# An attention and feed-forward kernel: the first stack loaded pair by pair, scores ahead of the first gate, and one gate and up pair moved into the first row

## What is computed

```python
xn = _layernorm(x, axis=-1)
x = x + _L0_attn_ref(xn, qkv_w, qkv_b, proj_w, proj_b) + _L0_ffn_ref(xn, w_gate, w_up, w_down)
# attention, 16 heads of 16 channels
qkv = xn @ qkv_w + qkv_b
attn = softmax(einsum('bnhd,bmhd->bhnm', q, k) * scale)
out = einsum('bhnm,bmhd->bnhd', attn, v) @ proj_w + proj_b
# feed-forward, hidden size 768, integer weights times 1/127
h = silu(xn @ wg.T) * (xn @ wu.T);  ffn = h @ wd.T
```

## Time and profile before

| | |
|---|---|
| median of 3 runs | 574.96 us |
| profiled execution | 576.71 us |
| its span | 574.9 us |
| PE, DVE, ACT, POOL busy | 97%, 81%, 73%, 53% of the span |
| mean granted clock of PE | 0.994 |

### The profile page before, as it was taken

The page is one execution under the profiler, slowest core; times in us unless marked ns, Lnnn a source line. Parts: engine busy times, 40 slices in busy tenths (PEclk is TensorE's granted clock), DMA queues, the critical chain, the costliest instruction groups (busy, mean ns, idle before and its releaser), DMA issues.

```text
span 574.9 us, 13815 instructions
## 1 busy us (share of the span) xinstructions
PE 555.6 (97%) x4844; PEld 334.2 (58%) x4844; DVE 464.9 (81%) x601; ACT 418.0 (73%) x573; POOL 305.1 (53%) x286
## 2 busy tenths in 40 slices
PE   7898899999999999999999999999999999998896
PEld 6656456565655557556665656555665556554453
DVE  5797777888878888888878889888978888788732
ACT  3666865888668975888668875788758886787572
POOL 3283536755564745755566554846467555355120
PEclk9899989999999999999999999999999999999999
DMA  8896086363854368371872449371873438520101
GB/s 235 254 244 146 3 216 179 57 141 118 236 110 105 62 198 206 56 164 71 245 143 69 98 156 241 62 156 29 228 189 61 93 138 227 99 57 21 57 2 38
DMA packets 55119, 74.89 MB, mean 130 GB/s; under 512 B 5680, under 2 KB 28208, under 8 KB 55088
## 3 DMA queue, kind: packets, MB, share of 16 engines
q1 hardware_dynamic: 55088, 74.47, 52.0%
HBM read 40.90 MB, written 33.03 MB: 129 GB/s over the span
## 4 chain that ended last, share of the span: by engine, by line
PE 90%; DVE 4%; ACT 3%; issue 1%; DMA 1%; SPq 0%; ACTq 0%
PE dense L1280 23%; PE o_bank L1254 22%; PE st_bank L1221 16%; PE dense L1324 14%; PE s_bank L1238 11%; PE dense L1264 2%; DVE neg_max L1004 1%; ACT probs L841 1%; PE dense L1393 1%; DMA probs<-in_L_attn_qkv_w 1%; PE dense L1380 0%; DVE w_dl L1033 0%; PE s_bank L1221 0%; ACT w_qkvh L830 0%; ACT probs L927 0%
## 5 line engine op out<-in xcount | busy, mean ns | idle before, releaser
L1004 DVE TENSOR_REDUCE neg_max<-s_bank 128x2 f32<-128x1024 f32 x250 | 304.9, 1220 | 73.9 <-PE s_bank L1238 72.8
L841 ACT ACTIVATE probs<-st_bank 128x1024 f32<-128x1024 f32 x250 | 256.4, 1026 | 112.6 <-PE st_bank L1221 109.4
L1254 PE MATMUL o_bank<-probs,v_ones 128*32 128x512 f32 x1024 | 137.1, 607 | 0.1
L1221 PEld LDWEIGHTS st_bank<-q_stack,k_stack 50*128 50x128 f32 x500 | 47.7, 184 | 131.7 <-ACT probs L841 82.1
L1221 PE MATMUL st_bank<-q_stack,k_stack 50*128 50x512 f32 x500 | 118.0, 466 | 5.3 <-ACT probs L841 5.0
L1238 PE MATMUL s_bank<-k_stack,q_stack 48*128 48x512 f32 x500 | 108.9, 429 | 0.9 <-DVE neg_max L1004 0.7
L742 POOL TENSOR_TENSOR hid_tl<-gated,hid_th 128x512 fp32r<-128x512 f32 x48 | 61.7, 1285 | 35.2 <-ACT hid_th L941 35.2
L736 POOL TENSOR_TENSOR gated<-gated,hid 128x512 f32<-128x512 f32 x48 | 61.7, 1285 | 28.7 <-DVE gated L1026 19.8
L1280 PE MATMUL dense<-xn_tl,w_gh 64*128 64x512 f32 x176 | 61.9, 391 | 0.0
L1280 PE MATMUL dense<-xn_tl,w_uh 64*128 64x512 f32 x176 | 61.9, 391 | 0.0
L1238 PEld LDWEIGHTS s_bank<-k_stack,q_stack 48*128 48x128 f32 x500 | 47.4, 185 | 20.7 <-DVE neg_max L1004 8.4
(11 more groups left out here) (152 smaller groups left out, 886.2 us busy)
## 6 DMA issues: line engine op xcount, KB each, us to landing
q_stack<-q_spread SPq DMA_DIRECT2D x64, 192.0 KB, 4.7
k_stack<-k_spread SPq DMA_DIRECT2D x64, 192.0 KB, 5.2
q_spread<-qk_parts SPq DMA_DIRECT2D x16, 512.0 KB, 3.8
k_spread<-qk_parts SPq DMA_DIRECT2D x16, 512.0 KB, 3.5
q_spread<-qk_parts SPq DMA_DIRECT2D x16, 256.0 KB, 4.1
k_spread<-qk_parts SPq DMA_DIRECT2D x16, 256.0 KB, 2.0
resid<-in_L_attn_x SPq DMA_DIRECT2D x16, 256.0 KB, 4.3
out<-resid SPq DMA_DIRECT2D x15, 256.0 KB, 2.2
```

Of the source, the lines that this page charges most:

```text
L841: nc.scalar.activation(probs[:, s % 2, 2 * half:2 * half + 2, :], transposed_bank(row, s, half)[:, :, :], ACT.Exp, scale=SCALE).then_inc(e ...
L1004: nc.vector.tensor_reduce(neg_max[:, g % 2, :, NT * pair + qt], score_bank(row, half)[:, :, :], AX_X, ALU.max, negate=True).then_inc(max_d ...
L1221: done = nc.tensor.matmul(transposed_bank(row, s, half)[:, r, :], k_stack[rows, pair, P * kt:P * (kt + 1)], q_stack[rows, pair, :], start= ...
L1254: done = nc.tensor.matmul(o_bank[32 * j:32 * (j + 1), :], v_ones[:, kt, 8 * (g // 2) + 2 * j + g % 2, :], probs[:, (s - 1) % 2, j, :], sta ...
```

## The change

Four edits. The first stack (group 0 of row 0) is loaded in two pairs with a semaphore each, eight transfers instead of four, and the scores wait for their pair only. The load of x for row 1 goes behind q's and k's spread writes instead of ahead of them. The first gate and up products go behind the first scores instead of ahead of them. The fourth gate and up leave the preparation for step 0 of row 0, which gets a table of its own: its ups stand in steps 0, 2 and 3, its q and k of index 0 in steps 5 and 6 (4 and 5 before), and its token split one step later.

```diff
+ROW0 = [
+    (0, 0, "up", KH + 3, 0, (2,)), (0, 0, "gate", KH + 3, 0, (0,)),
+    (1, 0, "v", 1, 0, (1, 2)),
+    (2, 0, "up", 4, 0, (1,)), (2, 0, "gate", 4, 0, (0,)), (2, 0, "max", 1, 0, (2,)),
+    (3, 0, "up", 5, 0, (2,)), (3, 0, "gate", 5, 0, (1,)),
+    (5, 0, "q", 0, 1, (1, 0)),
+    (6, 0, "k", 0, 1, (2, 1)), (6, 0, "max", 2, 0, (0,)),
+] + STEADY[STEADY.index((7, 0, "q", 1, 1, (2, 0))):]
...
-TOGETHER = {("up", i): ("gate", i) for i in range(KH)}
+TOGETHER = {("up", i): ("gate", i) for i in range(2 * KH)}
...
     (4, 0, "q", 1, 1), (5, 0, "k", 1, 1),
-    (7, 0, "gate", 0, 1), (8, 0, "up", 0, 1),
-    (10, 2, "gate", 1, 1),
-    (11, 2, "up", 1, 1),
+    (10, 1, "gate", 0, 1), (10, 2, "up", 0, 1),
+    (11, 1, "gate", 1, 1), (11, 2, "up", 1, 1),
     (12, 1, "wdown", 0, 1), (12, 1, "wdown", 1, 1), (12, 2, "gate", 2, 1),
     (13, 1, "wdown", 2, 1), (13, 2, "up", 2, 1),
-    (14, 1, "max", 0, 1), (14, 2, "gate", 3, 1),
-    (15, 1, "v", 0, 1), (15, 2, "up", 3, 1),
+    (14, 1, "max", 0, 1),
+    (15, 1, "v", 0, 1),
...
 TOKENS_SPLIT_AT = ((2, 1), (3, 1))
+ROW0_TOKENS_SPLIT_AT = ((3, 1), (4, 1))
...
     if like < 0:
         return FIRST
-
+    if like == 0:
+        return ROW0
...
+            def load_first_stack():
+
+                sp.wait_ge(ones_ready, 1)
+                for pair in range(2):
+                    for stack, parts in ((q_stack, q_spread), (k_stack, k_spread)):
+                        both = parts[0:P].rearrange("(p r e d) a n -> r e (d a) p n", p=2, r=2, e=2)[:, 0]
+                        for half in range(2):
+                            first = HALF * half
+                            sp.dma_start(stack[first:first + STACK, pair].bitcast(F32),
+                                         both[half][:, pair]).then_inc(first_stack_in[pair], 16)
...
                 if row.has(1):
                     spread_heads(row, "k", 0)
+                if row.like == -1:
+
+                    sp.wait_ge(dense_done, count(row, any_chunk, kind="xn", index=1))
+                    load_x(1)
...
-                if p == 0 and qt == 0:
-                    pe.wait_ge(stack_in[g], 16 * STACK_LOADS * (row.at + ahead + 1))
+                if g == 0 and row.like == -1:
+                    if qt == 0:
+                        pe.wait_ge(first_stack_in[p], 16 * STACK_LOADS)
+                elif p == 0 and qt == 0:
+                    pe.wait_ge(stack_in[g], 16 * STACK_LOADS * (row.at + ahead + (g > 0)))
```

More of the change, by code:

```diff
@@ L344, in build @@
         stack_in = [sem(f"stack_in{g}") for g in range(NG)]
+        first_stack_in = [sem(f"first_stack_in{pair}") for pair in range(2)]
         max_in = [sem(f"max_in{g}") for g in range(NG)]
@@ L456, in splits_at @@
                 return []
-            items = [("xn", n) for n in range(KC) if (step, slot) == TOKENS_SPLIT_AT[n] and row.has(0) and row.has(1)]
+            places = ROW0_TOKENS_SPLIT_AT if row.like == 0 else TOKENS_SPLIT_AT
+            items = [("xn", n) for n in range(KC) if (step, slot) == places[n] and row.has(0) and row.has(1)]
             if slot == 1:
@@ L591, in load_stack @@
             def load_stack(row, g):
-                if row.like == -1:
-                    sp.wait_ge(ones_ready, 1)
-                else:
+                if row.like >= 0:
                     sp.wait_ge(st_done, 2 * STEPS * row.at + 2 * NT * (g + 1))
@@ L643, in step @@
                     sp.dma_start(w_last, proj_w[P:2 * P]).then_inc(w_last_in, 16)
[L644 to L648, removed]
+                if row.has(0) and row.has(2):
                     if row.like == 0:
@@ L667, in step @@
                     heads_spread(row, 0)
+                if row.like == -1:
+                    load_first_stack()
+                elif row.has(1):
                     load_stack(row, 0)
@@ L741, in hidden_low @@
                 pool.wait_ge(hid_high, number(row, "up", m))
-                nc.gpsimd.tensor_tensor(hid_t[1][:, m, :], gated[:, m % 2, :], hid_t[0][:, m, :].bitcast(F32),
+                nc.gpsimd.tensor_tensor(hid_t[1][:, m % KH, :], gated[:, m % 2, :], hid_t[0][:, m % KH, :].bitcast(F32),
                                         ALU.subtract).then_inc(hid_low, 1)
@@ L940, in hidden_high @@
                 act.wait_ge(hid_product, number(row, "up", m))
-                nc.scalar.activation(hid_t[0][:, m, :], gated[:, m % 2, :], ACT.Copy).then_inc(hid_high, 1)
+                nc.scalar.activation(hid_t[0][:, m % KH, :], gated[:, m % 2, :], ACT.Copy).then_inc(hid_high, 1)
             def step(row):
@@ L1409, in spec_of @@
                 if kind == "up":
-                    return (banks, lambda h, a, k: (w_u, w_g)[h][a][:, k, tile(i)], lambda h, b, k: xn_t[b][:, k, :],
+                    return (banks, lambda h, a, k: (w_u, w_g)[h][a][:, k, tile(i % KH)], lambda h, b, k: xn_t[b][:, k, :],
                             terms_of(STATIONARY_EXACT if exact else SPLIT, KC))
```

## The result

The changed kernel took a median of **579.38 us** (578.99 to 580.23, 4 runs) beside 574.91 us for the kernel before (574.55 to 575.86, 4 runs): ratio 1.0077, 95% interval 1.0060 to 1.0095. That is slower, by 4.5 us where 1.4 had been forecast, and just above the upper end of the range. The profiled execution took 580.23 us, with a span of 578.3 us at a granted clock of 0.994. Run again on another chip, unchanged, the same kernel had a ratio of 1.0102 (1.0081 to 1.0123).

What follows compares the result with a forecast made beforehand. PE, busy 97% of the span, was taken as the bound, with VectorE at the preparation's end. The terms -2.4+0.6+3.2+0 = +1.4 gave profiled 578.1, median 576.4 us (forecast case, chance 0.35); range 573.2 to 579.2.

Steps and rivals of the forecast that it cites:

- First stack and x load: Preparation: first pair by about 23, first maximum about 26.5; 3 us slack, so the extra SP issues cost nothing.
- I estimate 0.7 us of VectorE gaps: End of the preparation: time given back because the first hidden tile stands behind 2.1 us of ScalarE work.
- End of the preparation: Decision 1.2 us earlier, at 44.0, then 1.2 us to the first product: row 0 starts at 45.2 instead of 47.58, -2.4 us.
- third rival: The rival "slower by more", chance 0.25; its second condition was thin work around the decision lowering the clock again, +1.45 us.
- Fourth pair in row 0: Row 0, steps 3 to 6: with the moved gate and up pair 15.5 us instead of 14.89, +0.6 us.
- k one step later: PE waits before transposed scores (8,0) for group 2's maxima, 2.2 to 3.7 us, taken as +3.2; late bound a 2.0 us landing.
- the later stack costs nothing behind the stall: Row 0: the next row's stack is later too, but PE asks for it in step 10, after the stall: nothing.
- Clock: Row 0: slow step 7 goes, but the lower level follows the wait in step 8: 0, between -1.45 and +1.45 us.
- slower by more: Timed runs before had no slow step 7, or thin work lowers the clock: 577.8 us, both 579.3; chance 0.25.

Runs made afterwards that it cites:

- trace with filled gaps: Changed kernel with idle PE transpositions, 8 before the first maxima's transposition and 20 before transposed scores (8,0), waits kept: 577.25 us, ratio 1.0054.
- second trace of the kernel before: The kernel before, run again unchanged for another trace: 574.5 us, ratio to itself 0.9998.
- trace of the preparation alone: Changed kernel without its row 0 table, the fourth gate and up back in the preparation: 575.20 us, ratio 1.0010 to the kernel before.
- run with v earlier: Changed kernel with the preparation's first v product in step 14 (slot 2) instead of step 15: 579.04 us, ratio 1.0082.

## Why the prediction was wrong

The direction and the main wait held. Two steps failed, the gain at the end of the preparation and the clock at nothing, and a third, the fourth pair in row 0, was sized too small.

Against the first trace of before, from which the sum was made, the changed kernel's trace gives: start -0.89 for -2.4, steps 3 to 6 +1.41 for +0.6, the wait 2.88 for 3.2, and the clock about -0.1 for 0 (step 7 -1.51; step 8 +0.85 beyond the wait; step 9 +0.57, against the row below). The 1.75 us that the median lay below the profiled time were carried over unchanged; after the change they are 0.85, and that is where the clock term's failure, told below, shows in this sum. So the miss of 3.0 us on the median is 1.5 and 0.8 and 0.9, less 0.3, to 0.1 us. Step 9 of the first trace of before:

```profile
81.83:87.00 5.17, 5.17 (x66) 3.85 (x64) 5.11 (x7) 4.16 (x6) 2.36 (x3) 1.00 1.04 236
```

The trace with filled gaps (span 575.0, clock 0.998) and the second trace of the kernel before (572.0, 1.000) allow a sum without the clock in it: start of row 0 46.37 to 44.81, -1.56; steps 3 to 6 14.90 to 16.30, +1.40; step 8 3.65 to 6.70, +3.05; the rest of the marks within 0.03. Together +2.9, and the spans differ by 3.0. Part of a start is scatter: four traces with the same new preparation reach its first product at 10.31 to 10.87 us, and the two kernels of this sum reach it at 10.54 and 10.31, so 0.2 of the 1.56 us need not be the change's.

**First stack and x load, nothing: right as far as it went.** The first pair was there at 23.55 for "about 23", and the first maximum came at 25.78 for "about 26.5". But an early first maximum turned out to be worth nothing. In the trace of the preparation alone, row 0 starts 1.0 us later than in the second trace of before, though the first maximum comes 1.0 us earlier (25.28 for 26.26):

```profile
47.34 0.47 PE L1304 MATMUL dense<-xn_th,w_uh 64*128 64x512 f32 x1 [0.78 <-ACT hid L916]
```

In the second trace of before VectorE goes without such gaps from the first maximum to 41 us. With the new order it waits for ScalarE three times (0.47, 0.31 and 0.37 us; in the changed kernel 0.53, 0.31 and 0.36, 1.20 in all, where the step "I estimate 0.7 us of VectorE gaps" had it), the wait before the fourth gate's half grows from 1.00 to 1.34 us, and the first gate's half now lies inside the chain instead of ahead of it.

**End of the preparation, -2.4: failed.** It measured -0.89 against the trace that it was worked out from. From the decision to the first product it took 1.30 us for the 1.2 taken; three other things were wrong. The given-back gaps were 1.20, not 0.7. The clock fell once more behind the thin work at 40 us (0.50 at 42 to 44 us), which lay in the third rival only ("the thin work around the decision lowers the clock once more"); with the gap filled row 0 starts at 44.81 (0.56 of the 1.88 us between the two traces are there at the first product already), so the term's 45.2 would about have stood at full clock. And the trace of before was itself 1.2 us late at that mark, by its own low stretch at 18 to 22 us; against the usual execution even 45.2 would have been -1.2. The sign of this last error could have been read: the earlier trace rows show 0.67 and 0.50, and the median lay 1.75 us below the profiled time.

**Fourth pair in row 0, +0.6: measured +1.4.** The pair's step (4.22 for 4.31) and the empty step (3.49) came as said, and k's 3.95 nearly so (3.86). The miss is q's step, 4.64 for 3.84: PE waited 0.61 us for POOL, which does the hidden tile's low part and the next product first, and the tokens' split had moved a step later as well. POOL's timeline of the changed kernel:

```profile
65.13 1.28 POOL L765 TENSOR_TENSOR hid_tl<-gated,hid_th 128x512 fp32r<-128x512 f32 x1 [1.07 <-ACT hid_th L964]
...
67.61 1.28 POOL L778 TENSOR_TENSOR xn_tl<-xn_blocks,xn_th 128x512 fp32r<-128x512 f32 x1
```

A step that the table moves carries its other engines' order with it.

**k one step later, +3.2: right.** The wait was 2.88 us, with filled gaps 2.95. From exponential (7,0), at 76.74 in the trace, to the issue of the second transfer it took 4.50 us (4.8 forecast), and from there 1.73 us to PE's start, between the two bounds of 0.51 and 2.0. (At the late bound the wait would have been 3.7 us, 0.5 above the 3.2 taken, where the prediction says 0.4.)

```profile
76.74 1.02 ACT L864 ACTIVATE probs<-st_bank 128x1024 f32<-128x1024 f32 x1 [0.62 <-PE st_bank L1244]
```

The sentence beside it, that the later stack costs nothing behind the stall, held; but with the stall taken away, the late chain of transfers made a wait of 2.5 us in step 12. The fixed cost of about 2.0 us that the Trainium skill, DMA: Bandwidth & Descriptors, section Anatomy of one DMA, gives (for transfers that GpSimd issues) is above the 1.73 us seen here for one that SP issued, and far below the 5.2 us behind full queues.

**Clock, 0: failed.** Against the first trace it came out at about 0 by luck: that execution had a slow step 7 to lose. The usual execution before has none, so nothing offset the stretch behind the wait; and there was a second one in the preparation. Both conditions of the rival "slower by more" came true; that its 579.3 lies so near to 579.38 is luck too, since it keeps the -2.4 and the +0.6. The rule of the Trainium skill, Perfetto Trace Analysis, section Matmul Optimizations, that the engine scales its power with utilization, agrees with the run that filled the gaps (1.00 at 42 to 44 us, where it had been 0.50). The chances (0.35 against 0.25) had these two the wrong way round, since the note that the timed runs lay 1.75 us below the profiled one already spoke for the rival.

## What to carry to other kernels

Before a stretch of a profile is priced, look whether that execution is a usual one: a profiled time above the median, with low-clock rows in it, makes a change look better than it is. Where a table moves one product, follow every queue that it passes to its end; as here, removing the first wait may only show the next one in the same chain, four steps on. And a gap has two prices, its length and the clock behind it, which idle matmuls in the gap tell apart.

## What was not expected of the hardware

Behind gaps of PE of 1.03 and 0.34 us, with 0.70 us of work between them, the granted clock fell to 0.50 (42 to 44 us); with eight idle transpositions, 1.09 us in all, in the first of them it stayed at 1.00. It also stayed at 1.00 behind a single gap of 1.23 us in the run with v earlier, where work followed without the second gap. A transfer of 8 KB took 1.73 us from its issue to the release of PE, and the like transfer of group 3 took 5.2 us when it stood behind stack loads at a DMA share of 1.06. A residual load of 256 KB, issued among the spreads, held POOL for 4.60 us.
